# The residual row is accumulated by TensorE instead of added by VectorE: output projection of a Mamba + MoE block

## The reference

```python
xn = layernorm(x)                                    # 8192 tokens x 128
x_, z = split(xn @ in_proj_w.T)                      # 256 + 256
x_ = silu(conv1d(x_, 4 taps) + conv_b)
dt, B, C = split(x_proj(x_))                         # per head, 16 + 16 + 16
delta = softplus(dt_proj(dt) + dt_proj_b)            # 256
s[t] = s[t-1] * exp(delta[t] * A) + delta[t] * x_[t] * B[t]     # 256 x 16 states
y[t] = sum_n s[t] * C[t] + x_[t] * Dskip
mamba = (y * silu(z)) @ out_proj_w.T                 # the output projection
moe = gate * (relu(tok @ W1 + b1) @ W2 + b2)         # at most 1024 tokens per expert
out = x + mamba + moe
```

## Time and profile before

| | |
|---|---|
| median of 3 runs | 1132.79 us (1132.73 to 1134.38) |
| the profiled execution's own time | 1134.47 us |
| its span | 1132.7 us |
| TensorE matmul, busy | 965.9 us, 85% |
| VectorE, busy | 1028.1 us, 91% |
| ScalarE, busy | 755.8 us, 67% |
| GpSimd, busy | 878.3 us, 78% |
| mean granted TensorE clock | 0.947 of full speed |

### The profile page before, as it was taken

How to read it: one execution, slowest core, us unless ns; L and a number is a source line. 1 busy time by engine, 2 the same in 40 slices (tenths; PEclk the granted TensorE clock), 3 DMA queues, 4 the chain that set the end, 5 groups by cost and what they waited for, 6 DMA issues and landing times.

```text
span 1132.7 us, 11797 instructions
## 1 busy us (share of the span) xinstructions
PE 965.9 (85%) x3525; PEld 442.5 (39%) x3525; DVE 1028.1 (91%) x1227; ACT 755.8 (67%) x1197; POOL 878.3 (78%) x730
## 2 busy tenths in 40 slices
PE   0676667898999999999999899999999999788786
PEld 0432213344444444444444444444444444333232
DVE  6856887999999999999999999999999999999996
ACT  2574642768777687778786877768777878576331
POOL 3305888779888898888988989889888888888753
PEclk9998867999999999999999999999999999899766
DMA  7528353443353345244324335333524332855500
GB/s 170 178 37 230 99 117 70 99 100 79 77 120 79 79 84 117 44 82 113 71 61 112 83 77 119 77 81 76 125 42 83 75 65 65 200 118 112 131 28 10
DMA packets 76095, 107.23 MB, mean 95 GB/s; under 512 B 13528, under 2 KB 43136, under 8 KB 76032
## 3 DMA queue, kind: packets, MB, share of 16 engines
q1 hardware_dynamic: 71936, 98.02, 39.7%
q0 software_dynamic: 4096, 8.46, 2.2%
HBM read 18.24 MB, written 21.10 MB: 35 GB/s over the span
## 4 chain that ended last, share of the span: by engine, by line
PE 32%; DVE 24%; issue 16%; ACT 15%; POOL 10%; DMA 1%; SPq 1%; POOLq 0%; DVEq 0%; ACTq 0%
DVE u_sb L926 10%; DVE s_sb L991 8%; PE bank L1156 5%; PE bank L1193 4%; PE bank L1121 4%; POOL s_sb L615 4%; PE bank L1101 4%; POOL expert_in L622 4%; PE bank L1208 4%; PE bank L1186 3%; ACT bank L808 3%; PE bank L1153 3%; ACT L713 2%; ACT L709 2%; PE bank L1112 2%
## 5 line engine op out<-in xcount | busy, mean ns | idle before, releaser
L615 POOL TENSOR_TENSOR s_sb<-s_sb,c_of 128x512 f32<-128x512 f32 x480 | 614.2, 1289 | 135.8 <-DVE s_sb L991 131.2
L991 DVE TENSOR_TENSOR_SCAN s_sb<-bank,u_sb 128x512 f32<-128x512 f32 x512 | 620.9, 1213 | 14.7 <-ACT bank L808 14.2
L808 ACT ACTIVATE bank<-bank,a_neg 128x510 f32<-128x510 f32 x512 | 332.2, 663 | 212.2 <-PE bank L1193 210.6
L926 DVE TENSOR_TENSOR u_sb<-bank,b_of 128x512 f32<-128x512 f32 x512 | 343.7, 671 | 37.7 <-PE bank L1186 36.9
L1186 PE MATMUL bank<-dsp,sel_d 128*128 128x512 f32 x512 | 328.6, 642 | 32.8 <-DVE u_sb L926 20.2
L1193 PE MATMUL bank<-dsp,sel_d 128*128 128x512 f32 x512 | 230.3, 450 | 51.4 <-DVE s_sb L991 48.5
L1186 PEld LDWEIGHTS bank<-dsp,sel_d 128*128 128x128 f32 x512 | 101.0, 197 | 211.0 <-DVE u_sb L926 107.9
L1193 PEld LDWEIGHTS bank<-dsp,sel_d 128*128 128x128 f32 x512 | 101.2, 198 | 177.3 <-DVE s_sb L991 131.7
L1208 PE MATMUL bank<-s_sb,con 128*32 128x512 f32 x1024 | 147.8, 651 | 23.1 <-POOL s_sb L615 20.2
L1101 PE MATMUL bank<-xnT,wx 128*128 128x512 f32 x256 | 132.3, 602 | 0.0
L622 POOL DMA_INDIRECT expert_in<-xn,put_at x64 | 65.3, 1020 | 18.0 <-issue 17.8
(11 more groups left out here) (144 smaller groups left out, 1034.4 us busy)
## 6 DMA issues: line engine op xcount, KB each, us to landing
b_of<-bc SPq DMA_DIRECT2D x64, 256.0 KB, 5.6
c_of<-bc SPq DMA_DIRECT2D x64, 256.0 KB, 6.0
dsp<-hi SPq DMA_DIRECT2D x64, 256.0 KB, 4.0
dsp<-dd SPq DMA_DIRECT2D x64, 256.0 KB, 4.6
expert_in<-fill SPq DMA_DIRECT2D x16, 260.0 KB, 3.3
xn<-expert_in SPq DMA_DIRECT2D x8, 520.0 KB, 5.3
moe<-fill SPq DMA_DIRECT2D x8, 512.0 KB, 6.5
xn<-L_ffn_W SPq DMA_DIRECT2D x16, 256.0 KB, 4.9
```

Of the source, the lines that this page charges most:

```text
L615: pool.tensor_tensor(s_now, s_now, c_of[:, hf, hh, :], ALU.mult).then_inc(S["p_ready"], 1)
L808: act.activation(d, d, ACT.Exp, scale=a_neg[:, k:k + 1]).then_inc(S["decay_ready"], 1)
L926: dve.tensor_tensor(u_sb[:, w % U_RING, :], du_ps[w % 2][:, :], b_of[:, hf, head_of(w), :], ALU.mult).then_inc(S["u_ready"], 1)
L991: dve.tensor_tensor_scan(s_sb[:, w % S_RING, :], decay_of(w)[:, :], u_sb[:, w % U_RING, :], 0.0, ALU.mult, ALU.add).then_inc(S["scan_done" ...
```

## The change

The residual row is put into the bank by an identity matmul, with `start=True`, ahead of the projection's matmuls, in all 16 chunks; the expert rows of the last three chunks come next, then the projection's own. The bank then holds the finished sum, and ScalarE copies it over the rows in `acc` at its slot 21; for the last chunk it does so after its loop. VectorE's `add_out` and its semaphore are gone.

```diff
-OUT_PROJ = (1, (18, 19), "dve", 20)
+OUT_PROJ = (1, (18, 19), "act", 21)
...
-        for by in ("act", "dve", "bc"):
+        for by in ("act", "bc"):
...
+            def take_out(ch):
+
+                act.wait_ge(S["misc_pe"], tile_made("outp", ch, 0, 0))
+                act.activation(acc[:, ch * CT:(ch + 1) * CT, :],
+                               tile_bank("outp", ch, 0, 0)[:, :].rearrange("p (i d) -> p i d", d=DM), ACT.Copy
+                               ).then_inc(S["misc_act"], 1)
...
+                        elif x.kind == "outp":
+                            take_out(x.of)
+            take_out(CHUNKS - 1)
...
-            def add_out(ch):
-
-                rows = acc[:, ch * CT:(ch + 1) * CT, :]
-                dve.wait_ge(S["misc_pe"], tile_made("outp", ch, 0, 0))
-                dve.tensor_tensor(rows, tile_bank("outp", ch, 0, 0)[:, :].rearrange("p (i d) -> p i d", d=DM), rows,
-                                  ALU.add).then_inc(S["misc_dve"], 1)
...
-                    for x in reads_at.get(t, []):
-                        if x.kind == "outp":
-                            add_out(x.of)
...
-            add_out(CHUNKS - 1)
...
                 for i in range(CT // 2 * part, CT // 2 * (part + 1)):
+                    mm = pe.matmul(t[:, i * P:(i + 1) * P], ident, acc[:, ch * CT + i, :], start=True, stop=False)
+                    if more:
+                        mm = pe.matmul(t[:, i * P:(i + 1) * P], ident, back[:, ch * CT + i, :],
+                                       start=False, stop=False)
                     for hf in range(HALVES):
                         mm = pe.matmul(t[:, i * P:(i + 1) * P], g_sb[:, hf, i * P:(i + 1) * P], wo[:, hf, :],
-                                       start=(hf == 0), stop=(hf == HALVES - 1 and not more))
-                    if more:
-                        mm = pe.matmul(t[:, i * P:(i + 1) * P], ident, back[:, ch * CT + i, :],
-                                       start=False, stop=True)
+                                       start=False, stop=(hf == HALVES - 1))
```

More of the change, by code:

```diff
@@ L223, in bass_mamba_moe @@
             "scattered du_spread delta_spread u_ready decay_ready scan_done p_dve p_ready sum_done "
-            "skip_added g_ready misc_pe misc_act misc_dve misc_bc b_loaded0 b_loaded1 c_loaded0 c_loaded1 sp_act sp_chain "
+            "skip_added g_ready misc_pe misc_act misc_bc b_loaded0 b_loaded1 c_loaded0 c_loaded1 sp_act sp_chain "
             "dx_ready dd_ready hi_ready lo_ready stacked ffn_loaded0 ffn_loaded1 moe_put0 moe_put1 moe_put2 "
```

## The result

The changed kernel takes 1137.29 us (median of 11 runs, 1135.76 to 1140.54), the kernel before 1133.98 in the same runs; ratio 1.0033, 95% interval 1.0024 to 1.0042. It is slower, by 2.7 to 4.8 us. The forecast was 1132.5, a change of -0.3; measured is +3.3. One execution of the study, in f3, took 1186.03 us at a granted clock of 0.82 and is left out of every number.

What follows compares the result with a forecast made beforehand. No single engine was taken as the bound: who is late was read slot by slot, with TensorE full in chunks 3, 6, 9, 12. Terms -3.0 - 1.2 + 3.6 - 0.5 + 0.8 = -0.3 us gave 1132.5; range 1128.3 to 1138.0.

Steps and rivals of the forecast that it cites:

- VectorE's gain at u(22): With the add gone, u(22) starts 0.6 us earlier in chunks 1, 4, 7, 10 and 0.3 in 2, 5, 8, 11.
- 13 to 15 together: Last three chunks: chunk 13 gains 0.6 us like the light ones, chunk 14 gains 0.3, chunk 15 gains 0.2.
- tail: After the last gate: four more identity matmuls cost 0.9 us, shorter copy returns 0.1; +0.8, other end 1.6.
- the copy hidden: ScalarE's copy of about 0.61 us, ahead of slot 22's exponential, was costed at nothing.
- the mechanism in the full chunks: Chunks 3, 6, 9, 12: tight links pass TensorE's added 0.9 us through ScalarE to VectorE; +3.6 us.
- A: VectorE bounds throughout: 15 adds give 0.60 us each, tail costs 0.8; -8.2 us, 1124.6; chance 0.08.
- B: The loss in chunks 3, 6, 9, 12 is made up, nothing instead of +3.6; -3.9 us, 1128.9; chance 0.17.
- D: ScalarE's copy doesn't hide: 0.6 us in the 8 chunks with most expert work; +4.5 us, 1137.3; chance 0.04.
- at delta(25) TensorE had waited 0.24 for the scan and so follows VectorE, 0.3 earlier: Chunks 2, 5, 8, 11: TensorE keeps up with the earlier VectorE, so each gains 0.3 us, -1.2 in all.
- level by then: Chunks 1, 4, 7, 10: TensorE absorbs its added 0.9 us by delta(25), so VectorE keeps 0.6 each.
- rival C: From delta(25): chunks 2, 5, 8, 11 lose 0.9, first kind gains nothing; +6.9, or +4.5 (1137.3) first half only; chance 0.24.
- its own sign: The prediction called itself wrong if the total time moved by over 2.3 us either way.

Runs made afterwards that it cites:

- f3: The kernel before plus one unused 128x512 matmul in TensorE's pause in chunks 3, 6, 9, 12: 1133.99 us, ratio 1.0003.
- g1: The changed kernel run once more, on another chip, beside the kernel before: 1139.54 us, ratio 1.0052.
- f1: The changed kernel plus one unused 128x512 matmul in TensorE's pause in chunks 3, 6, 9, 12: 1136.61 us, ratio 1.0029.
- g2: The changed kernel plus the unused matmul in the pause of chunks 3, 6, 9, 12, run again on another chip: 1136.71 us, ratio 1.0027.
- e2: The changed kernel without its identity matmuls on acc's rows (residual left out of the output), copy kept, no VectorE add: 1130.62 us, ratio 0.9975.
- e1: The kernel before, VectorE's add kept, plus four identity matmuls per chunk that are overwritten: 1142.82 us, ratio 1.0075.
- f4: The kernel before, VectorE's add kept, plus two identity matmuls per chunk that are overwritten: 1138.40 us, ratio 1.0044.
- g3: The changed kernel with the last two projections (in chunk 15 and behind the loop) as in the kernel before: 1137.93 us, ratio 1.0039.
- e3: The changed kernel, but in chunks 3, 6, 9, 12 VectorE adds as before: 1133.43 us, ratio 0.9992.
- e4: The kernel before with the accumulation and its copy only in chunks 1, 4, 7, 10, 13: 1131.87 us, ratio 0.9983.
- h1: Same as e4, but GpSimd adds the last chunk's expert rows ahead of time instead of four tail identity matmuls: 1131.48 us, ratio 0.9976.

## Why the prediction was wrong

Its terms, as put, against the table. "Regular" is a value without a fall of the clock in chunks 3, 6, 9, 12; the four traces with the full change are changed, g1, f1 and g2.

| step | forecast | measured, regular |
|---|---|---|
| VectorE's gain at u(22), chunks 1, 4, 7, 10 / 2, 5, 8, 11 | -0.6 / -0.3 | -0.56 / -0.28 at the slot |
| what is left of it at the chunk's end, 1, 4, 7, 10 | -0.6 each, -2.4 | -0.34 to -0.43, -1.6 |
| the same, 2, 5, 8, 11 | -0.3 each, -1.2 | +0.01 to +0.05, +0.1 |
| 3, 6, 9, 12 | +0.9 each, +3.6 | +0.86 to +0.92, +3.6 |
| 13 to 15 together | -1.1 | -0.4 (mean of four, -1.5 to +0.1), not told from the clock |
| tail | +0.8 | +1.1 |
| falls of the clock, slot 28 of 3, 6, 9, 12 | none | 1.1 to 1.7 each time |

**Right:** the identity pair at 0.22 us; the copy hidden (e2); the gain at u(22); and the mechanism in the full chunks, TensorE to ScalarE to TensorE to VectorE, with its price to 0.05 us. e1 and f4 show that it is TensorE's work alone and proportional to it. Rivals A, B and D are out: VectorE waits for TensorE, chunks 3, 6, 9, 12 do grow, and the copy is free.

**Failed, first: "at delta(25) TensorE had waited 0.24 for the scan and so follows VectorE, 0.3 earlier", and "level by then" for the light chunks.** I took a wait that is there before the change as proof that TensorE would still wait after it. What is needed is a budget: all that TensorE can catch up from the added work to the start of the next burst, against 0.9 us. In the changed kernel TensorE has no idle time from du(22) to du(26) in chunks 7 and 8: it catches up as much as it can. In chunk 8 that is 0.88 us (7.83 us from du(22) to du(26) before, 6.95 now), though the profile shows 0.32 us of idle time there before. So du(26) is level with where it stood, and VectorE, 0.27 early, waits for the burst at the chunk's end. In chunk 7 it is 1.29 us (7.94, now 6.65; 0.56 shown idle), du(26) comes 0.38 early, and that is what the chunk keeps of 0.56. This was rival C's place, but not its price: its chunks come out at 0 and -0.4, not at +0.9 and 0. The two terms were 2.1 us too good.

**Failed, second, and nowhere in the text: the longer pause.** Through chunk 9 TensorE is 0.9 us late, and so is ScalarE's run, but the last scan that TensorE waits for before the pause is only 0.37 late. So the pause grows by the difference, from 1.18 to 1.72 us. It isn't only VectorE's gain that does this: in e1 VectorE keeps its add, and the pause is as long. Chunk 9 of e1, the start of ScalarE's run, that scan and the pause:

```profile
731.52 0.69 ACT L731 ACTIVATE sp_a<-bank,small 128x512 f32<-128x512 f32 x1
...
732.75 1.21 DVE L991 TENSOR_TENSOR_SCAN s_sb<-bank,u_sb 128x512 f32<-128x512 f32 x1
...
737.95 2.69 PE L1154 MATMUL bank<-xn 128*128 128x512 f32 x3 [1.72 <-ACT xn L762]
```

and the scan in the kernel before and in the changed one:

```profile
729.89 1.22 DVE L991 TENSOR_TENSOR_SCAN s_sb<-bank,u_sb 128x512 f32<-128x512 f32 x1
...
731.88 1.21 DVE L994 TENSOR_TENSOR_SCAN s_sb<-bank,u_sb 128x512 f32<-128x512 f32 x1
```

From the start of ScalarE's run to the scan it was 1.77 us (728.12 to 729.89), and is 1.24 in the changed kernel (from 730.64), 1.23 in e1 and in e2. VectorE had stood 0.54 us behind what TensorE and ScalarE allowed. Less work for VectorE or more for TensorE takes this slack away, and the pause gets it.

In the traces the clock fell behind the pause in 10 of 20 passages at 1.72 to 1.73 us (changed 2, g1 2, e1 3, e2 2, g3 1, of four each) and 2 of 4 at 1.64, in 0 of 16 at 1.16 to 1.20 (before, e3, e4, h1), and in 0 of 16 with the filler (0.87 and 0.34). That the pause is the cause is shown by the fillers: they add work and take the falls away. The forecast weighed the clock only in chunk 15 and the tail.

**Sized wrong, or not told: the tail and chunks 13 to 15.** From the start of the last gate step to the read of the finished bank it is 6.59 to 7.34 us in five traces with the new tail (changed, g1, f1, g2, e3), 5.65 to 6.03 in four with the old one (before, f3, e4, g3): +1.2 between the means, and 0.1 less by the shorter copy, where +0.8 was forecast. For chunks 13 to 15 the terms were -0.6 and -0.5, and the traces can't confirm either. In chunk 13 the table has -1.1, but -0.7 of it stands in e1 and f4 as well, where VectorE gains nothing, and g3, with the change in that chunk, has +0.2; in f3 and g3 the clock's low stretches begin as in before's trace, in the others not. In chunks 14 and 15, the projections of e4 and h1 are as before, and the two traces show +1.5 and -0.1.

The regular terms give -1.6 + 0.1 + 3.6 - 0.4 + 1.1 = +2.8 us. The kernel with the filler, where the clock doesn't fall behind the pause, has +3.2 and +2.9. The changed kernel adds 0.1 to 2.8 by the clock. So nothing of size is unexplained; how often the clock falls in the executions whose trace was not kept is open.

The measured 1137.29 us lies inside the stated range of 1128.3 to 1138.0 and next to the 1137.3 of rivals C (first form) and D. That is luck: C had chunks 2, 5, 8, 11 at +0.9 each and D the copy at 0.6, and the runs show 0.0 and nothing for them. By its own sign, a move of over 2.3 us, the prediction is wrong.

## What to carry to other kernels

Work moved to another engine is paid where that engine has no room: look at it stretch by stretch, and set the added time against all that it can catch up before the next burst, not against the one wait nearest by. The idle times in the profile are a lower bound of that: 0.32 us were shown in chunk 8 and 0.88 caught up. The distances between the starts of the same matmuls, where they wait and where they don't, tell more. A wait in the trace is a budget that the first edit spends. The same edit can be worth keeping in some iterations only: here four light chunks gain 0.4 us each and four full ones lose 0.9.

## What the runs showed of the hardware

- A pause of TensorE of 1.72 us in a stretch at 2.4 GHz was followed by 1.2 GHz in 10 of 20 passages, one of 1.16 to 1.20 us in none of 16. With one useless matmul of 0.87 us in the pause the clock held in all 16 passages; in the kernel before that matmul cost nothing that could be measured (1.0003).
- A float32 identity matmul of 128x128 costs 0.22 us at the full clock and 0.43 us at the low one; four more of them made the tail 1.2 us longer up to the read (means of traces), four fewer 1.3 shorter (h1 against e4, one trace each).
- A ScalarE copy of a 128x512 bank (598 ns) is shorter than VectorE's add of the same bank (685 ns).
